# Two cross attentions: q, k, v and outputs per head in place of folded weight products, scores and outputs on 64x64 quarters

## The reference

```python
def _L1_xattn_ref(x, context, Wq, Wk, Wv, Wo, bo):
    q = (x @ Wq).reshape(B, Nq, HEADS, DIM_HEAD).transpose(0, 2, 1, 3)
    k = (context @ Wk).reshape(B, Nc, HEADS, DIM_HEAD).transpose(0, 2, 1, 3)
    v = (context @ Wv).reshape(B, Nc, HEADS, DIM_HEAD).transpose(0, 2, 1, 3)
    sim = jnp.einsum('bhid,bhjd->bhij', q, k) * SCALE
    attn = jax.nn.softmax(sim, axis=-1)
    out = jnp.einsum('bhij,bhjd->bhid', attn, v)
    out = out.transpose(0, 2, 1, 3).reshape(B, Nq, HEADS * DIM_HEAD)
    return out @ Wo + bo
x = x + jnp.tanh(g_xattn[0]) * _L0_xattn_ref(_layernorm(x, axis=-1), ctx_768, ...)
x = x + jnp.tanh(g_ffn[0]) * _L0_ffn_ref(_layernorm(x, axis=-1), ...)
x = x + jnp.tanh(g_xattn[1]) * _L1_xattn_ref(_layernorm(x, axis=-1), ctx_768, ...)
x = x + jnp.tanh(g_ffn[1]) * _L1_ffn_ref(_layernorm(x, axis=-1), ...)
```

## Time and profile before

| | us |
|---|---|
| median of 3 runs | 1917.74 |
| lowest and highest | 1917.61, 1919.73 |
| span of the profiled execution | 1918.0 |
| first scores of the first attention, last | 24.4, 316.0 |
| first scores of the second attention, last | 1300.4, 1783.2 |
| mean granted clock of PE, of full speed | 0.980 |

### The profile page before, as it was taken

One profiled execution on the slowest core, in us unless ns is written; L12 is line 12 of the kernel. 1 busy time (PEld: TensorE's weight loads), 2 busy tenths in 40 slices (PEclk: granted clock), 3 DMA queues, 4 the chain that ended last, 5 costly groups with the idle time before them and its releaser, 6 DMA issues. The chain is left out here.

```text
span 1918.0 us, 72744 instructions
## 1 busy us (share of the span) xinstructions
PE 1812.8 (95%) x28635; PEld 1311.9 (68%) x28635; DVE 1609.1 (84%) x3645; ACT 1564.4 (82%) x2773; POOL 662.4 (35%) x918
## 2 busy tenths in 40 slices
PE   6999998896999999999999999998999999999898
PEld 4777776542666666666666666766777777777677
DVE  5999987598788888888888888778999999988744
ACT  5899997575998989898989989876888888888543
POOL 4788887231000000000000000004666666655565
PEclk8999999897999999999999999999999999999899
DMA  7644545495000000000000001004665555533233
GB/s 180 130 99 93 103 94 102 139 364 187 14 11 15 13 14 11 15 13 15 10 14 14 13 12 52 2 2 107 153 169 154 144 156 147 154 69 72 64 111 121
DMA packets 312954, 160.67 MB, mean 84 GB/s; under 512 B 236558, under 2 KB 295862, under 8 KB 312374
## 3 DMA queue, kind: packets, MB, share of 16 engines
q1 hardware_dynamic: 312278, 157.95, 31.4%
q10 hardware_dynamic: 480, 0.05, 0.0%
HBM read 62.33 MB, written 36.83 MB: 52 GB/s over the span
## 5 line engine op out<-in xcount | busy, mean ns | idle before, releaser
L1793 DVE TENSOR_TENSOR h<-g,h 128x1024 f16<-128x1024 f32 x256 | 313.3, 1224 | 138.3 <-ACT h L1725 138.0
L239 PEld LDWEIGHTS psE<-ew,h 128*128 128x128 f16 x6144 | 351.2, 98 | 56.0 <-issue 40.1
L239 PE MATMUL psE<-ew,h 128*128 128x128 f16 x6144 | 365.2, 219 | 12.8 <-DVE eo L1803 6.0
L1720 ACT ACTIVATE g<-psH,eb1T 128x512 f32<-128x512 f32 x512 | 330.2, 680 | 30.9 <-PE psH L239 24.5
L814 POOL TENSOR_TENSOR Ph<-E,Ph 128x512 f16<-128x512 f32 x192 | 222.0, 1156 | 235.9 <-ACT Ph L768 235.9
L1866 POOL MEMSET rbias<- 64x384 f32 x1 | 0.4, 411 | 839.2 <-POOLq L133 839.2
L1725 ACT ACTIVATE h<-g 128x1024 f16<-128x1024 f32 x256 | 270.6, 1057 | 8.1
L720 ACT ACTIVATE vB<-psV 128x512 f16<-128x512 f32 x384 | 225.9, 589 | 51.2 <-PE psV L618 49.0
L841 DVE TENSOR_TENSOR vB<-psV,vB 128x512 f16<-128x512 f32 x384 | 248.4, 678 | 1.1 <-ACT vB L720 1.0
L618 PE MATMUL psV<-shared 96*64 96x512 f16 x1536 | 209.9, 379 | 1.5 <-DVE vB L841 1.5
L820 POOL TENSOR_TENSOR E<-E,rden 128x512 f32<-128x512 f32 x192 | 199.7, 1040 | 15.1 <-DVE rden L852 14.3
(11 more groups left out here) (308 smaller groups left out, 3417.9 us busy)
## 6 DMA issues: line engine op xcount, KB each, us to landing
keys_ahead<-shared SPq DMA_DIRECT2D x52, 512.0 KB, 4.8
shared<-keys_ahead SPq DMA_DIRECT2D x52, 512.0 KB, 3.6
rawe<-in_L_ffn_w_dram SPq DMA_DIRECT2D x32, 256.0 KB, 3.1
wb<-rw SPq DMA_DIRECT2D x64, 128.0 KB, 2.0
rows<-places SPq DMA_DIRECT2D x110, 64.0 KB, 2.5
out_dram<-x SPq DMA_DIRECT2D x7, 512.0 KB, 3.2
context_T<-shared SPq DMA_DIRECT2D x64, 48.0 KB, 2.4
PT<-Ph SPq DMA_TRANSPOSE x192, 2.8
```

What stands on the lines that cost most here:

```text
L239: last = e.matmul(to, a, b, start=start and n == 0, stop=stop and n == 2, **flags)
L1720: e.activation(g32[:, ft, :], psH[:, ft, :], ACT.Gelu_apprx_tanh, bias=b1T[:, a.expert(1) * FT + ft:a.expert(1) * FT + ft + 1]).then_inc(s ...
L1793: e.tensor_tensor(h[:, 1 - par, 1, 2 * q:2 * q + 2, :], g32[:, 2 * q:2 * q + 2, :], h[:, 1 - par, 0, 2 * q:2 * q + 2, :], ALU.subtract)\
```

## The change

The weight products go. Both attentions form for each unit q (from x) and k (from the context) with 48 matmuls into `psQK`, in two halves (`project(0)`, `project(1)`), and copy each half to the fp32 tile `QK`; in the first attention DVE copies the second half, in the second ACT. The tokens are now kept as high and low parts (`xT`, with a DVE subtraction). Scores of a head are q times k over 64 numbers: 16 fp32 matmuls of 64 columns, each with 64 input rows and 64 output rows, in turn on the four quarters of the array, into two banks of `psS`. Values per head are 12 matmuls of 256 columns (were 12 of 512), with one ACT copy and one DVE subtraction a unit (were two and two). Outputs per head `psO` are 48 fp16 matmuls of 64 columns on quarters; ACT copies them to fp32 (`O32`), and `psY` is 8 fp32 matmuls of 128 columns with Wo. The output step trails by one unit more (`a5`), and DVE's maximum, subtraction and sum each come one body later. On POOL the scaling now comes ahead of the low part of the same unit.

`keys_ahead` holds k of all 16 heads of a tile in the same 8 blocks, so in the first 52 tiles the second attention forms only q (24 matmuls a unit) and needs the load before the tile's first unit. `select_tokens` splits Wk, Wq and Wv into parts with 4 steps on ACT and 4 on POOL, and writes them out; `run_experts` loads these parts and Wo at its end, behind the wait that stood there. The first block only loads and splits.

```diff
-    cT1 = shared[0:DC, 64 * D:64 * D + 8 * P].rearrange("p (r h t) -> p r h t", r=4, h=2)
-    u1 = shared[:, 64 * D + 8 * P:64 * D + 8 * P + 6 * 8 * P].bitcast(F32).rearrange("p (s h l) -> p s h l", s=3, h=8)
+    WQ1 = shared[:, 0:16 * P].rearrange("p (l g k d) -> p l g k d", l=2, g=2, k=4)
+    WK1 = shared[0:DC, 16 * P:32 * P].rearrange("p (l g k d) -> p l g k d", l=2, g=2, k=4)
+    WV1 = shared[0:DC, 32 * P:48 * P].rearrange("p (l g h k) -> p l g h k", l=2, g=2, h=2)
+    WO1 = shared[:, 48 * P:64 * P].bitcast(F32).rearrange("p (g k h d) -> p g k h d", g=2, k=2, h=2)
+    cT1 = shared[0:DC, 64 * P:72 * P].rearrange("p (r h t) -> p r h t", r=4, h=2)
+    KL1 = shared[:, 72 * P:104 * P].bitcast(F32).rearrange("p (s k l) -> p s k l", s=2, k=8)
+    O1 = shared[:, 104 * P:120 * P].bitcast(F32).rearrange("p (s h k) -> p s h k", s=2, h=2)
     xna1 = shared[:, 120 * P:124 * P].bitcast(F32).rearrange("p (k d) -> p k d", k=2)
...
-                last.then_inc(s["wT"], 1)
-                e.wait_ge(s["wT_scalar"], 2 * g + 2)
-                e.wait_ge(s["wT_vector"], g + 1)
-                if g:
-                    e.wait_ge(s["fold_lo"], 2 * g)
-                for pair in range(4):
-                    for hp in range(2):
...
+                        def project(part):
+
+                            pairs = range(4) if a.ahead else range(2 * part, 2 * part + 2)
+                            todo = [(wq, xT[:, a.tp], k) for k in pairs]
+                            if not a.ahead:
+                                todo += [(wk, cT[:, a.ring], k) for k in pairs]
+                            for q, (w, moving, k) in enumerate(todo):
+                                for n, (wl, ml) in enumerate(PASSES):
                                     for m in range(2):
-                                        last = e.matmul(psU[half(m), b, to], AT[:, al, a.g, h, half(m)],
-                                                        cT[:, a.ring, cl, :], start=n == 0, stop=n == 2)
-                            last.then_inc(s[f"U{b}"], 1)
-
-                        nx = Unit(j, -1) if first else a
-
...
+                                wait(e, s["uc1"], a.formed() - 1)
+                            else:
+                                wait(e, s["uc0"], a.j - 1)
+                            project(0)
+                        if a3.on:
+                            wait(e, s["vl"], a3.j - 1)
+                            for b in range(2):
+                                for n, (bl, cl) in enumerate(PASSES):
+                                    for hp in range(2):
+                                        last = e.matmul(psV[half(hp), 256 * b:256 * b + 256], cT[:, a3.ring, cl, half(b)],
+                                                        wv[:, bl, a3.g, hp, :], start=n == 0, stop=n == 2)
+                            last.then_inc(s["V"], 1)
+                        if nx.opens:
+                            wait(e, s["ln"], nx.t)
+                            wait(e, s["xl"], nx.t - 1)
+                            if first:
+                                wait(e, s["ct"], nx.t - 1)
+                            for m in range(2):
+                                last = e.matmul(psX[half(m)], xn[:, nx.tp, half(m)], ident32[:], start=True, stop=True)
+                            last.then_inc(s["X"], 1)
+                        if a.on and not a.ahead:
+                            wait(e, s["uc0"], a.j)
+                            project(1)
+                        if a5.on:
+                            wait(e, s["oc"], a5.j)
+                            if a5.opens:
+                                wait(e, s["res"], a5.t - 1)
+                            for hp in range(2):
+                                for k2 in range(2):
                                     for b in range(2):
...
-                        else:
-                            ready()
+                                        last = e.matmul(psY[half(b), 0:D],
+                                                        O32[:, a5.par, hp, P * k2 + 64 * b:P * k2 + 64 * b + 64],
+                                                        wo[:, a5.g, k2, hp, :], start=a5.g == hp == k2 == 0,
+                                                        stop=a5.g == G - 1 and hp == k2 == 1)
+                            last.then_inc(s["Y"], 1)
                         if first and nx.on:
+                            e.wait_ge(s["cc_pad"], 1)
+                            wait(e, s["clo"], nx.t)
+                            wait(e, s["xl"], nx.t)
                             for hl in range(2):
                                 for m in range(2):
                                     last = e.transpose(psC[half(m), hl, :], cc[:, nx.tp, hl, half(m)], ident16[:])
                             last.then_inc(s["C"], 1)
+                        if a4.on:
+                            wait(e, s["vl"], a4.j)
+                            wait(e, s["oc"], a4.j - 1)
+                            wait(e, s[f"pt{a4.par}"], ring_of(a4.j, 2, a4.par), 16)
+                            e.sem_inc(s["O_begins"], 1)
+                            for k2 in range(2):
+                                for b in range(2):
+                                    to = slice(P * k2 + 64 * b, P * k2 + 64 * b + 64)
+                                    for n, (vl, pl) in enumerate(PASSES):
+                                        for hp in range(2):
+                                            for kp in range(2):
+                                                k = 2 * k2 + kp
+                                                last = e.matmul(psO[half(kp), hp, to],
+                                                                vB[half(hp), a4.par, vl, b, DH * k:DH * k + DH],
+                                                                PT[half(hp), a4.par, pl, k, half(b)],
+                                                                start=n == 0, stop=n == 2)
+                            last.then_inc(s["O"], 1)
                         if a.on:
-                            if a.opens:
-                                wait(e, s["xt"], a.t)
-                            if a.loaded:
-                                wait(e, s[f"ul{a.tp}"], ring_of(a.t, 2, a.tp), 16)
+                            if a.ahead:
+                                if a.opens:
+                                    wait(e, s[f"ul{a.tp}"], ring_of(a.t, 2, a.tp), 16)
+                                wait(e, s["uc0"], a.j)
+                            else:
+                                wait(e, s["uc1"], a.formed())
                             wait(e, s["sub"], a.j - 1)
-                            for h in (0, 4):
-                                if not a.loaded:
-                                    wait(e, s[f"uc{h // 4}"], a.key())
+                            e.sem_inc(s["S_begins"], 1)
+                            for k in range(4):
+                                keys = KL1[:, a.tp, 4 * a.g + k] if a.ahead else QK[:, a.par, 1, k]
                                 for b in range(2):
-                                    last = e.matmul(psS[half(b), h:h + 4, :], xT[:, a.tp, half(b)],
-                                                    u[:, a.slot, h:h + 4, half(b)], start=True, stop=True)
...
+                def projected(e, a, part, copy):
+
+                    wait(e, s["S"], a.j - 2)
+                    wait(e, s[f"U{part}"], a.j if part == 0 else a.formed())
+                    if a.ahead:
+                        to, frm = QK[:, a.par, 0].rearrange("p k t -> p (k t)"), psQK[:]
+                    else:
+                        to = QK[:, a.par, :, 2 * part:2 * part + 2].rearrange("p q k t -> p q (k t)")
+                        frm = psQK[:].rearrange("p (q k) -> p q k", q=2)
+                    copy(to, frm).then_inc(s[f"uc{part}"], 1)
 
                 @block.scalar
...
-                                            vB[:, a.par, 0, b].rearrange("p k d -> p (k d)"), ALU.subtract)\
-                             .then_inc(s["vl" + name], 1)
-
+                        a, a1, a2, a3, a5, nx = (Unit(j, k) for k in (0, 1, 2, 3, 5, -1))
+                        by_head = "p (k h) n -> p h k n"
+
+                        if a2.on:
+                            wait(e, s["exp"], a2.j)
+                            wait(e, s["mul"], a2.j - 2)
+                            e.tensor_reduce(den[:, a2.par, :], E[:, a2.four], AX.X, ALU.add).then_inc(s["den"], 1)
+                            wait(e, s["den"], a2.j)
+                            e.reciprocal(rden[:, a2.par, :], den[:, a2.par, :]).then_inc(s["rden"], 1)
+                        if a1.on:
+                            scores = psS[:, :, 0:256].rearrange("p h (k n) -> p h k n", n=N)
+                            wait(e, s["S"], a1.j)
+                            e.tensor_reduce(top[:], scores, AX.X, ALU.max).then_inc(s["max"], 1)
+                            wait(e, s["max"], a1.j)
```

(29 more changed lines are left out.)

537 lines of the change are left out of this document (169 added, 368 removed).

## The result

The changed kernel takes 2109.35 us (median of four, 2103.16 to 2110.51), the kernel before 1918.6: a ratio of 1.0986, 95% interval 1.0969 to 1.1003. It is slower by 191 us. The forecast was 1914, the range ended at 1990.

What follows compares the result with a forecast made beforehand. PE was taken to bound both attentions, with DVE taking over the first. First attention +1, loaded keys -19, formed keys -3, instruction fetch +17, edges 0: -4 on 1918 gives 1914 us; 8 in 10 range 1870 to 1990.

Steps and rivals of the forecast that it cites:

- the term for the instruction fetch: Second attention's first loop, 8.6 blocks, 11 jumps back: each waits 1.5 us for a block (bounds 0 and 3), +17 us.
- Rival 1: Second attention's first loop is kept without refetch: 17 us less, about 1897, or 1880 with faster quarters; chance 0.26.
- Quarters: Scores and outputs on the array's four quarters, both attentions: 0.50 and 0.45 us, together 0.95 a unit.
- the changes of shape: Each unit goes to quarters and back on PE, 0.09 us a change: 0.19 us a unit, possibly down to nothing.
- Rival 2: Small matmuls on quarters keep a slower pace of their own: +182, about 2096, or halfway +67, about 1981; chance 0.19.
- rival 3: Input halves do not overlap, so scores and outputs run on two blocks at a time: +132, about 2046; chance 0.08.
- The unit of the second attention: Two units with loaded keys take PE 6.98 us for 7.35, waits included: 52 x -0.37 = -19 us.
- DVE takes over: First attention: DVE at 4.36 us a unit against PE's 4.34, taken as 4.43, so nothing is gained: +1 us.
- the 18 counted: First-attention units where three more small DVE steps no longer fit under PE: +0.3 us each.
- Formed keys: Second attention, two units with formed keys: 8.36 us for 8.57, 12 x -0.21 = -3 us.
- The new second loop runs one round and jumps back nowhere: Second attention's second loop, in the instruction fetch estimate: no jump back, so no fetch cost was added.
- The middle and the tail: Selection and experts left at their time, 0; edges: first block -3, tails of both attentions +3.

Runs made afterwards that it cites:

- new_straight: The changed kernel with PE's loaded-key stage of the second attention (104 units) written out without a loop; 2046.25 us in one run.
- new_rounds4: The changed kernel with the second attention's loaded-key stage looped over 4 units instead of 8 on all engines; ratio 1.0267, single times 1968 to 1983 us.
- old_rounds16: The kernel before with only PE's loop over the second attention's loaded-key stage in rounds of 16 units instead of 8; 1970.98 us, ratio 1.0266.

## Why the prediction was wrong

**The failed step is the term for the instruction fetch**, and with it the forecast as a whole. It was named, counted (8.6 blocks, 11 jumps) and given a sign, and the recorded range ended far below the result because of its size: +17 for 131 measured. Two errors are in it. A jump was priced at 1.5 us, from how long a block's packet occupies its DMA and how soon a small transfer lands, with an upper bound of 3. Measured are 4.1 to 5.1 us of idleness and 2.1 more at the lower clock; the packet takes 1.1 us of that, and the start of the fetch and the time from the packet to the first instruction are in no row that was used. And the round between the jumps was taken as free. No bound was put on it, although the number of instructions in a unit was at hand: 276 in 3.5 us leave 3.2 us for a block, while before it was 6.4. That the clock falls behind idle stretches shows in the trace of before too (0.66 on average in 442 to 460 us, where PE is busy in 4.2 of 18 us) and was not added either.

The Trainium skill (Runtime: NRT & Kernel Launch, Instruction fetch mechanics) says that a taken branch to a target outside the current window of two pages forces a fetch before PE can go on. The runs agree on the fetch, with 4.1 to 5.1 us, and not on the window: loops of 6.1 and 6.5 blocks run without one. Nor are the 2048 instructions that the prediction took from that section the border, since one of 1953 is fetched again. The same section of the Trainium skill also calls the cost of crossing a block mostly hidden; at 6.4 us a block that holds, at 3.4 it does not, and new_straight shows 0.82 us a unit for it.

**Rival 1 (the loop stays at hand)** did not come true in the change, but new_rounds4 is that case and refutes its price as well: 1968 to 1983, not 1897 or 1880. The 131 us of the loop came back; the gain of the quarters did not.

**Quarters.** Forecast 0.50 and 0.45 us, and 0.19 for the changes of shape. In the first attention the scores measure 0.63 and the outputs 0.45, 1.08 together for 1.14; 0.10 of the scores' time belongs to the change of shape behind them (the gap to the next step is 0.15, for 0.05 between like shapes). The starts show four blocks at work: four outputs start within 10 ns, and groups of four follow each other every 31 ns, 7.8 ns for one. Rival 2 (a pace of 23 to 25 ns) and rival 3 (two blocks only) are refuted by it. Rival 2's time, 2096, lies near the result for a reason it did not have.

**The unit of the second attention**: forecast 6.98 for two, measured 7.39 (new_rounds4), for 7.35 before. Start to start: q 0.69 for 0.67, values 0.66 for 0.65, projection with its change of shape 0.97 as forecast, scores 0.63 for 0.60, turned tokens as forecast; outputs 0.57 for 0.45. The last is most of what can be named; 0.13 of the two units lie at the jump back and before a key load. The 48 outputs take their 0.38 there too, but the scores start 0.19 us after the last of them, 0.07 in the first attention and among formed keys, though what they wait for was done long before. Why was not found. The whole forecast gain of -19 is gone: 104 units at +0.04 are +4 in its place, and 6 more us lie in units 0 to 15 of new_rounds4, which include its first, fetched round.

**The first attention**: forecast +1, measured +24. "DVE takes over" was wrong: PE paces the undisturbed unit at 4.53 (forecast for PE 4.34). q and k in two halves cost 1.38 for 1.34, turned tokens 0.26 for 0.22, and the turned context 0.24 for 0.11, since it now stands between two changes of shape. That is +0.02 on 4.51 in those units. Units beside norm steps or a jump cost 0.1 to 1.6 us more, and there are more of them than the 18 counted: some 30 of 47 lie above 4.6 us, 13 us in all over units 16 to 62. The other 11 us fall in units 0 to 15. There PE waits some 8 us for instructions, in written-out code and in its loop's first round: units 8 to 11 take 5.97 on average and units 12 to 15, for which no block comes, 4.97. And it waits 9 us for results of DVE and ACT, 4 in the kernel before; the longest, 4.1 us, is for the low part of the tokens, a DVE step that the change brought.

**Formed keys**: forecast -3, measured +13. The unit is 4.36 us when nothing waits, for 4.18 forecast; 28 blocks came in 110 us there, 3.9 us each, and 322 instructions a unit make 4.9. Against the kernel before (4.28) the unit's own time is +2 us in all, and most of the other 11 are waits for instructions. "The new second loop runs one round and jumps back nowhere", counted as free, was the place where written-out code should have been priced.

**The middle and the tail**: forecast 0 and 0 net of edges, measured +9.5 and +3. Of the 9.5, some 4.6 lie at the start of the second attention, in a wait of the step behind the first turned tokens (L585, at 1326.29) that the view puts down to "issue" (PE's row, then DVE's):

```profile
1331.63 1.49 PE L554 MATMUL psQK<-xTa,shared 128*64 128x128 f16 x24 [4.64 <-issue]
```

```profile
1331.24 0.28 DVE L798 TENSOR_TENSOR xTa<-psXC,xTa 128x128 f16<-128x128 f32 x1
```

It is no wait for instructions: no packet comes on q8 between 1311.0 and 1332.5 us. q needs the low part of the turned tokens (`wait(e, s["xl"], a.t)`), and in DVE's program that new step stands behind the statistics and norm steps, which run from 1326.26 to 1331.3 us; PE goes on 0.1 us after it. The kernel before formed its keys from the context at that place and waited for nothing there. The change put a DVE step into PE's path at the start of the attention, and the prediction's middle, taken as 0, had no term for it. The other 5 us are as much as traces of the kernel before and of its variants with 52 tiles differ among themselves in this stretch (983 to 989 us), so no more is said of them.

## What to carry over

Count the engine's instructions, not only its time: divide the instructions of a stretch by its time, and where a block of 256 would last less than the fetch takes, code outside a kept loop is bound by its own fetch. Here blocks of 3.4 us were, in a stage where one came every 4.1 to 4.2 us, and blocks of 3.5 us where one came every 3.9; blocks of 3.7 us there and of 6.4 us in the kernel before were hardly or not. Keep PE's loop bodies under about 1,660 instructions when a change splits matmuls into smaller ones; halving the round was worth 131 us here, and doubling it in the kernel before cost 50. Small matmuls on quarters run side by side as fast as hoped and still gave nothing here: with the loop kept, two units take 7.39 us for 7.35. Each brings two instructions (four in fp32), and each change of shape 0.1 us. A step that moves to another engine needs a look at the start of each stage too, where that engine's program is full of other steps: it cost 4.6 us here.

## What the runs showed of the hardware

- The packet of PE's next block starts 1.55 us after the one before is entered, and PE can use the block 2.70 us after that (means over 62 waits in the kernel after, spread 0.2 to 3.6 and 2.2 to 4.4): 4.12 us a block in the loop, 4.19 written out, 3.9 among formed keys. A jump into a block that is not kept idles PE for 4.1 to 5.1 us (ten jumps). In old_rounds16 each jump brings two waits, 4.70 and 3.55 us with four matmul records between them at the one shown, which fits a target near a block's end.
- PE's loops of 5.3, 6.1 and 6.5 blocks ran round after round without a packet on its queue; one of 7.6 was fetched in every round.
- Behind such a wait PE's granted clock is at the lower of its two levels, 0.50 of full speed, for 4.2 us (1614.0 to 1618.2), which costs 2.1.
- Where blocks are fetched other transfers land later: transposes in 2.9 to 3.4 us for 2.7. PE's waits for them grew by 10 us when the loop of the kernel before was written out, which cost 13.5 us in all.
- Four 64x64 fp16 matmuls on the four quarters start within 10 ns of each other, the next four 31 ns later.
